# Two feed-forward layers: local attention's turns in another order, the second norm and the gated unit in one block, shifted copies by transfer

## The reference

```
def _layer(x, wqkv, qs, ksc, wo, lg, lb, w1, b1, w2, b2):
    h = shift_token(x)                     # channels 64..127 come from the token before
    q, k, v = split(h @ wqkv)              # 8 heads of 64
    q, k = l2norm(q) * qs, l2norm(k) * ksc
    q, k = rotary_xpos(q, k)
    o = local_attention(q, k, v)           # blocks of 64 tokens see themselves and the block before
    x = x + o @ wo
    h = shift_token(x)
    h = (h - mean(h)) / sqrt(var(h) + 1e-5) * lg + lb
    a, g = split(h @ w1 + b1)              # 341 each
    return x + (a * gelu(g)) @ w2 + b2
```

## Time and profile before

| | us |
|---|---|
| median of 3 runs (lowest, highest) | 1972.62 (1968.84, 1976.20) |
| the profiled execution | 1974.57 |
| its span | 1972.8 |
| layer 0: attention, norm, gated unit | 1098 to 1435, to 1461.2, to 1533 |
| layer 1: attention, norm, gated unit | 1533 to 1870, to 1897.7, to 1972.8 |

### The profile page before, as it was taken

How to read it: one execution, slowest core, us unless ns; L and a number is a source line. 1 busy time by engine, 2 the same in 40 slices (tenths; PEclk the granted TensorE clock), 3 DMA queues, 4 the chain that set the end, 5 groups by cost and what they waited for, 6 DMA issues and landing times. The chain is left out here.

```text
span 1972.8 us, 68063 instructions
## 1 busy us (share of the span) xinstructions
PE 1765.5 (89%) x28076; PEld 1051.8 (53%) x28076; DVE 1112.6 (56%) x3304; ACT 1487.9 (75%) x2649; POOL 425.4 (22%) x351
## 2 busy tenths in 40 slices
PE   8888899999999999999998788888879688888888
PEld 5664555555555555555554355555633355555533
DVE  5444533333333333333311699999853698989754
ACT  3333699999998999999998478887833587877733
POOL 1004000000000000000000556565300665565200
PEclk9988999999998999999999899998999899999999
DMA  1000311111111111111101201010000010010000
GB/s 56 3 3 24 113 51 53 59 46 58 50 56 42 58 58 58 59 58 46 42 16 55 57 18 25 16 23 14 17 1 0 20 25 18 18 23 13 18 11 32
DMA packets 42339, 69.60 MB, mean 35 GB/s; under 512 B 7377, under 2 KB 33105, under 8 KB 42065
## 3 DMA queue, kind: packets, MB, share of 16 engines
q1 hardware_dynamic: 42064, 65.66, 10.6%
HBM read 21.08 MB, written 2.10 MB: 12 GB/s over the span
## 5 line engine op out<-in xcount | busy, mean ns | idle before, releaser
L653 ACT ACTIVATE x_probs<-x_pss 128x1024 f32<-128x1024 f32 x832 | 806.4, 1021 | 51.7 <-PE x_pss L574 35.5
L588 PE MATMUL x_acc<-x_probs,x_v 128*32 128x256 f32 x6656 | 437.9, 380 | 0.1
L574 PE MATMUL x_pss<-x_qx,x_kx 32*128 32x256 bf16 x9984 | 348.4, 270 | 14.1 <-issue 6.3
L574 PEld LDWEIGHTS x_pss<-x_qx,x_kx 32*128 32x128 bf16 x9984 | 221.4, 93 | 199.8 <-ACT x_probs L653 180.3
L588 PEld LDWEIGHTS x_acc<-x_probs,x_v 128*32 128x32 f32 x6656 | 206.6, 110 | 93.5 <-issue 9.4
L1245 ACT ACTIVATE l_prob<-l_sim,l_neg_top,l_inv_norm 128x128 f32<-128x128 f32 x512 | 245.3, 485 | 0.4
L700 DVE COPY x_vnext<-x_psp 128x128 f32<-128x128 f32 (+1 forms) x199 | 59.1, 297 | 315.4 <-PE x_psp L552 312.3
L873 POOL TENSOR_TENSOR l_turned_half<-l_raw,l_tabB 128x512 f32<-128x512 f32 x128 | 160.2, 1272 | 155.7 <-ACT l_raw L1197 155.7
L629 POOL COPY x_zq<-zT 128x256 f32 (+1 forms) x15 | 6.0, 401 | 763.6 <-PE x_psp L559 695.4
L1149 DVE TENSOR_TENSOR l_prob<-l_prob,l_inv_total 128x512 f32<-128x512 f32 x128 | 157.5, 1231 | 4.4
L883 POOL TENSOR_TENSOR l_direct<-l_direct,l_turned_half 128x1024 f32<-128x1024 f32 x64 | 150.8, 2356 | 0.0
(11 more groups left out here) (172 smaller groups left out, 2826.7 us busy)
## 6 DMA issues: line engine op xcount, KB each, us to landing
x_kx<-x_kp SPq DMA_DIRECT2D x96, 208.0 KB, 2.3
x_cT<-in_context SPq DMA_DIRECT2D x16, 832.0 KB, 4.5
x_qx<-x_qp SPq DMA_DIRECT2D x48, 192.0 KB, 3.1
l_vmid<-l_vt SPq DMA_DIRECT2D x64, 128.0 KB, 2.3
xT<-in_x SPq DMA_DIRECT2D x8, 256.0 KB, 5.2
shifted<-zT SPq DMA_DIRECT2D x32, 64.0 KB, 2.0
out_x<-xT SPq DMA_DIRECT2D x8, 256.0 KB, 2.0
shifted<-zT SPq DMA_DIRECT2D x32, 63.8 KB, 2.0
```

The source lines that it names most:

```text
L574: ins = pe.matmul(pss[bank(k, 2 * p + r // 2)][:, r % 2, e, :], kx[par][rows, g, j * P:(j + 1) * P], qx[par][rows, g, a * S:(a + 1) * S], ...
L588: ins = pe.matmul(acc[32 * r:32 * r + 32, 0:S], v[:, j, g, r, :], probs[SLOT[p]][r // 2][:, r % 2, e, :], start=(u == 0), stop=(u == UNITS ...
L653: act.activation(probs[SLOT[p]][y][:, :, :, :], pss[bank(k, 2 * p + y)][:, :, :, :], ACT.Sigmoid, scale=HD ** -0.5).then_inc(weighed, 1)
```

## The change

**Local attention.** The `turn` of PE, ACT, DVE and POOL lists the same pieces in another order; some move to a neighbouring turn, as `mask(x, 0, 0)`, which is now the last of the turn before. `turn_halves` gets a wait on `joined`, since it may now run ahead of the join that reads its tile. SP gets `shift_sum`: once a row's sum is in `zT`, two transfers write its shifted copy into `hs` (`moved_to`). POOL clears the first token's upper half once per layer.

```
@@ local_attention, SP
+            def shift_sum(n):
+                sp.wait_ge(added, n + 1)
+                sp.dma_start(moved_to[0:64, n * S:(n + 1) * S], zT[0:64, n * S:(n + 1) * S]).then_inc(moved[n // 2], 16)
+                sp.dma_start(moved_to[64:P, n * S + 1:(n + 1) * S], zT[64:P, n * S:(n + 1) * S - 1]).then_inc(moved[n // 2], 16)
             for n in range(B):
                 middle(n)
                 if n + 4 < B:
                     shift(n + 4)
+                if n >= 3:
+                    shift_sum(n - 3)
+            for n in range(B - 3, B):
+                shift_sum(n)
@@ POOL
             def turn(x):
+                turn_halves(later(x, 1), 1)
+                join(later(x, 1), 0)
+                turn_halves(later(x, 2), 0)
                 scale_keys(later(x, 1), 0)
-                turn_halves(later(x, 2), 0)
                 join(later(x, 1), 1)
                 scale_keys(later(x, 1), 1)
-                turn_halves(later(x, 2), 1)
-                join(later(x, 2), 0)
@@ PE, the new order
+                score(x, 0)
+                project_q(later(x, 2), 0)
+                project_k(later(x, 2), 0)
+                project_v(x, 1)
+                turn_over(later(x, -1), 1, 0)
+                project_q(later(x, 2), 1)
+                value(later(x, -1), 0)
+                turn_over(later(x, -1), 1, 1, x)
+                score(x, 1)
+                value(later(x, -1), 1)
+                flip_q(later(x, 1), 0)
+                turn_over(x, 0, 0)
+                project_k(later(x, 2), 1)
+                project_out(later(x, -1))
+                flip_k(later(x, 1), 0)
+                flip_q(later(x, 1), 1)
+                turn_over(x, 0, 1)
+                flip_k(later(x, 1), 1)
+                project_v(later(x, 1), 0)
@@ DVE, the new order
+                norm(later(x, -1), 1, 1)
+                multiply_q(later(x, 2), 0)
+                multiply_k(later(x, 2), 0)
+                copy_v(x, 1)
+                mask(x, 0, 1)
+                floor_of(later(x, 1))
+                norm(x, 0, 0)
+                multiply_q(later(x, 2), 1)
+                inverse_norms(later(x, 1))
+                mask(x, 1, 0)
+                sums(later(x, 2), 0)
+                mask(x, 1, 1)
+                multiply_k(later(x, 2), 1)
+                norm(x, 0, 1)
+                place_keys(later(x, 1), 0)
+                add(later(x, -1))
+                norm(x, 1, 0)
+                place_keys(later(x, 1), 1)
+                sums(later(x, 2), 1)
+                copy_v(later(x, 1), 0)
+                mask(later(x, 1), 0, 0)
@@ ACT, the new order
+                exps(later(x, -1), 1, 1)
+                copy(later(x, -1), 0, 1)
+                copy_q(later(x, 2), 0)
+                copy_k(later(x, 2), 0)
+                exps(x, 0, 0)
+                squares(later(x, 2), 0)
+                copy_q(later(x, 2), 1)
+                copy(later(x, -1), 1, 0)
+                roots(later(x, 1))
+                copy_out(later(x, -1), 0)
+                copy(later(x, -1), 1, 1)
+                exps(x, 0, 1)
+                copy_out(later(x, -1), 1)
+                copy_k(later(x, 2), 1)
+                place_queries(later(x, 1), 0)
+                exps(x, 1, 0)
+                squares(later(x, 2), 1)
+                copy(x, 0, 0)
+                place_queries(later(x, 1), 1)
```

```
@@ norm_and_gate, PE (new)
+            fold()
+            for n in range(6):
+                mean_of(n)
+            variances(0)
+            for n in range(6, NCH):
+                mean_of(n)
+            variances(1)
+            pe.wait_ge(newton, run * NG * 2 + 2)
+            for c in range(4):
+                spread_out(0, c)
+            pe.wait_ge(newton, (run * NG + 1) * 2 + 2)
+            pe.wait_ge(centered, base + NCH)
+            chunks(pe, chunk)
+            narrow(NCH - 1, 1)
@@ its helpers
+            def mean_of(n):
+                pe.wait_ge(moved[n], 16 + 64 * (layer + 1))
...
+            def fold():
+                for m in range(2 * HC):
+                    ins = pe.matmul(wide[3][:, m:m + 1], w["w1"][:, m * P:(m + 1) * P], w["ln_b"][:, 0:1], start=True, stop=True)
+                ins.then_inc(folded, 1)
...
+            def widen(n, c):
+                if isinstance(n, int) and n == 0:
+                    pe.wait_ge(normed, base + (1, 1, 6)[c])
+                else:
+                    pe.wait_ge(gate_ready, passes + HC * (n - 1) + c + 1)
...
+            def chunk(n, u):
+                if isinstance(n, int) and n == 0:
+                    widen(0, 0)
+                    for c in range(4):
+                        spread_out(1, c)
+                    widen(0, 1)
+                    widen(0, 2)
+                else:
+                    if isinstance(n, int) and n == 1:
+                        pe.wait_ge(normed, base + NCH)
+                    widen(n, 0)
+                    narrow(n - 1, 1 - u)
+                    widen(n, 1)
+                    widen(n, 2)
@@ DVE (new)
+            dve.wait_ge(folded, layer + 1)
+            dve.tensor_tensor(bias[:, :], wide[3][:, 0:2 * HC], w["b1"][:, :], ALU.add).then_inc(bias_ready, 1)
+            for n in range(NCH):
+                dve.wait_ge(mean_ready, base + n + 1)
+                dve.tensor_tensor(hs[:, at[n]], hs[:, at[n]], mean[n % 2][:, :], ALU.subtract).then_inc(centered, 1)
+            refine(0)
+            scale(0)
+            refine(1)
+            for n in range(1, NCH):
+                scale(n)
+            chunks(dve, chunk)
+            add(NCH - 1)
```

More of the change, by code:

```diff
@@ L908, in _, with project_q @@
         def _(pe):
[L909 to L911 removed]
+            def project_q(x, t):
                 if exists(x):
@@ L1327, in narrow @@
             def narrow(n, u):
-                pe.wait_ge(gate_ready, HC * (n + 1))
-                if not isinstance(n, int) or n > 0:
-                    pe.wait_ge(added, n)
+                pe.wait_ge(gate_ready, passes + HC * (n + 1))
+                if isinstance(n, int) and n == 0:
+                    pe.wait_ge(normed, base + NCH)
+                else:
+                    pe.wait_ge(added, runs + n)
                 for c in range(HC):
@@ L1343, in _ @@
+            pe.wait_ge(newton, (run * NG + 1) * 2 + 2)
+            pe.wait_ge(centered, base + NCH)
             chunks(pe, chunk)
             narrow(NCH - 1, 1)
-        @block.scalar
-        def _(act):
-            with act.Fori(0, NCH) as n:
-                for c in range(HC):
-                    act.wait_ge(up, HC * n + c + 1)
-                    act.activation(gelu[c][:, :], psg[c][:, :], ACT.Gelu,
-                                   bias=w["b1"][:, HC + c:HC + c + 1]).then_inc(gelu_ready, 1)
@@ L1375, in chunk, with _, square_of, guess @@
                         add(n - 1)
-                    if c == 1 and (not isinstance(n, int) or n < NCH - 1):
-                        shift_by_bias(n + 1)
-            shift_by_bias(0)
+            dve.wait_ge(folded, layer + 1)
[8 more added lines that the diff above has]
+                scale(n)
             chunks(dve, chunk)
             add(NCH - 1)
+        @block.scalar
+        def _(act):
+            def square_of(n):
+                act.wait_ge(centered, base + n + 1)
+                act.activation(square[n][:, :], hs[:, at[n]], ACT.Square).then_inc(square_ready, 1)
+            def guess(g):
+                act.wait_ge(var_ready, run * NG + g + 1)
+                act.activation(rstd[g][:, :], var[g][:, :], ACT.Ln, bias=eps[:, 0:1]).then_inc(log_ready, 1)
+                act.wait_ge(log_ready, run * NG + g + 1)
+                act.activation(rstd[g][:, :], rstd[g][:, :], ACT.Exp, scale=-0.5).then_inc(guess_ready, 1)
+                act.wait_ge(guess_ready, (run * NG + g) * 2 + 1)
+                act.activation(rsquare[g][:, :], rstd[g][:, :], ACT.Square).then_inc(guess_ready, 1)
+            act.preload_act_table_set("natural_log_exp_and_others")
+            for n in range(6):
+                square_of(n)
+            guess(0)
+            for n in range(6, NCH):
+                square_of(n)
+            guess(1)
+            act.preload_act_table_set("gelu_and_others")
+            act.wait_ge(bias_ready, layer + 1)
+            with act.Fori(0, NCH) as n:
+                for c in range(HC):
+                    act.wait_ge(up, passes + HC * n + c + 1)
+                    act.activation(gelu[c][:, :], psg[c][:, :], ACT.Gelu,
+                                   bias=bias[:, HC + c:HC + c + 1]).then_inc(gelu_ready, 1)
 def build(nc, a, out):
@@ L1397, in build @@
         made = ctx.enter_context(nc.semaphore("made"))
+        moved = [ctx.enter_context(nc.semaphore(f"moved{n}")) for n in range(NCH)]
+        stored = ctx.enter_context(nc.semaphore("stored"))
+        gates = [ctx.enter_context(nc.semaphore(f"gate_{n}")) for n in (
+            "folded", "bias_ready", "up", "gelu_ready", "gate_ready", "down", "added")]
```

155 lines of the change are left out of this document (71 added, 84 removed).

## The result

| | us |
|---|---|
| median before (lowest, highest) | 1972.62 (1968.84, 1976.20) |
| median after (lowest, highest) | 1877.65 (1873.96, 1877.82) |
| ratio, 95% interval | 0.9513 (0.9479 to 0.9547) |
| profiled execution after, its span | 1873.96, 1872.1 |

The forecast was 1889, its range 1860 to 1935. The kernel became 11 us faster than forecast. Lines have moved: `norm` is now L1146 and L1148, `neg_top` L1138, the last `inverse_norms` L1119, `add` L1156; POOL's `turn_halves` L870, `join` L880, `scale_keys` L889; in the joint block the mean is L1336, `fold` L1341, the subtraction L1442, `widen` L1359, `narrow` L1370, the sum into `zT` L1424.

What follows compares the result with a forecast made beforehand. DVE was taken as the bound, held up by POOL's instructions in flight. Norm and gated unit 23.8, looped turns 55.9 and part-empty turns 4 sum to 83.7 us off 1974.6, 1890.9; median forecast 1889 us, range 1860 to 1935.

Steps and rivals of the forecast that it cites:

- 4.0 us of blocking a turn: Looped attention turns, layer 0: DVE operations with two SBUF inputs wait for POOL's instruction in flight, 4.0 us a turn.
- Part B: Looped attention turns: new orders shorten a turn from 20.18 and 20.28 to 17.9 us, gaining 55.9 us.
- norm(n,1,0): In the turn, due where POOL's first half-turn ends: loses 0.05 us meeting that boundary, 1.25 if not; taken as 0.65.
- Heads and tails: First four and last three attention turns, part empty: gain 2 us per layer, 4 in all (0 to 12).
- Part A: Norm and gated unit of both feed-forward layers: gain 23.8 us, from 20 to 27.
- One half-clock stretch per norm: First up products of the joint block: PE at half clock, some 1.7 us, kept in a gain of 7.2 us.
- its 8.8: Layer 1's norm: gain 8.8 us, since that norm is 1.5 us longer before the change.
- A second stretch per norm: Joint block without warm-up products: another slow PE stretch in each norm, making the gain there 20.4 instead of 23.8 us.
- ACT as the bound (1858): Looped turns: POOL's work falls almost wholly in the gaps, ACT bounds at 16.6 us a turn; 1858 us, chance 0.15.
- PE's clock on the path (1923): Looped turns: half clock ahead of products feeding ACT costs 1.4 us, turn 19.3, or blocking stays near 3; chance 0.23.
- The rivals with 3 us or more of blocking (1945, 1971): Turns: POOL's shorter groups block as much, 20.2 us, chance 0.07; or meet nearly all ten operations, 21.3 us, chance 0.05.
- random meetings: Upper case for the turn: ten sensitive DVE operations meet POOL at random, each losing 0.50 us, 5.0 in all; turn 21.3.

Runs made afterwards that it cites:

- the joint block alone: Changed kernel with the old orders of the turns, keeping only the joint block of norm and gated unit with shifted copies by transfer: 1952.2 us, ratio 0.9905.

## Why the prediction was right, and where it was off

**What bounds the kernel.** Right: DVE, by 4.0 us of blocking a turn. With POOL cut away the turn loses 3.75 us of its 4.0 blocked in layer 0 and 3.5 for 3.3 in layer 1. DVE's own work stays at 15.2 to 15.6 us a turn in every kernel here, and blocked and idle time make up the rest.

**Part B, the turn.** The forecast was 15.3 own + 1.0 idle + 1.6 blocked = 17.9. Layer 0: (196.34 - 10.9)/12 = 15.5 own, (204.30 - 196.34)/12 = 0.7 idle, 0.9 blocked, 17.0. The blocking was mis-sized by 0.7 us: all `neg_top` together took 0.29 a turn (priced at 0.5), norm(n,0,1) 0.17 (0.3), and norm(n,1,0) 0.45 (0.65): five misses at 1.07 over twelve turns. The norms and `inverse_norms` expected in POOL's pauses did lie there. Layer 1: 15.5 own, 1.3 idle, 1.0 blocked, 17.8. Of the idle 0.5 is two stalls. DVE stood 3.00 us and 2.84 us at the first norm's reciprocal. The second, and what the instruction queue did from 1677 to 1685:
```profile
1679.14 0.18 DVE L1146 RECIPROCAL l_inv_total<-l_total 128x4 f32<-128x4 f32 x1 [2.84 <-issue]
...
q14 instruction: 3, 0.02, 0.9%
```
The exponentials that this norm reads had ended by 1676.2, and nothing in the trace released it. PE then stood 3.54 us and took 2.07 instead of 1.12 for its next product; the turn took 22.75 us, the same turn of layer 0 16.85. Both stalls lie in the turn in which the loop goes back. All nine kernels here with the new order of DVE have two of 2.5 to 3.1 us, at that reciprocal, in layer 1 alone. With the old order it is `sums` that stands there, 1.2 to 2.2 us, twice in layer 1 (the joint block alone has none). In both orders that is the first piece of the turn, whatever it computes. An instruction fetch is my guess; layer 0 has packets on such queues too, without a stall, and no run tried it.

**Heads and tails.** Forecast 4, measured 7.3, nearly all of it in the heads. The 3.2 us ahead of the first feed-forward layer are in code that the change doesn't touch.

**Part A.** Right: 22.4 for 23.8. The steps of the joint block, by the timeline:
```profile
1390.80 1.47 PE L1341 MATMUL g_wide<-w_ln_b,w_w 128*128 128x1 f32 x12 [2.28 <-PEq L755]
...
1393.27 0.69 DVE L1442 TENSOR_TENSOR hs<-hs,g_mean 128x512 f32<-128x512 f32 x1 [0.80 <-PE g_mean L1336]
...
1427.91 0.75 DVE L1424 SCALAR_TENSOR_TENSOR zT<-g_wide,w_b,zT 128x512 f32 x1 [1.32 <-PE g_wide L1370]
1435.76 0.75 DVE L1424 SCALAR_TENSOR_TENSOR zT<-g_wide,w_b,zT 128x512 f32 x1 [1.33 <-PE g_wide L1370]
```
The last `add` ends at 1388.98: the first subtraction is 4.29 us later (forecast 4.3), `fold` 1.47 us (1.5), chunks are 7.85 apart (7.86). One half-clock stretch per norm was kept in the sum and one came per layer: in layer 0 at 1407.12, in layer 1 at the block's start, where the first three subtractions are 1.7 us apart. There the last subtraction is 3.1 us later behind the `add` than in layer 0; less the stretch that doesn't come behind it, that cost layer 1 about 1.5 us of its 8.8. Where such a stretch falls differs from trace to trace, and the old blocks vary too (97.9 to 100.4 us in layer 0): by the means of all traces part A is worth 12.2 + 11.1 = 23.3 us. A second stretch per norm did not come. The prediction's 20.4 us, worked out from the Trainium skill ("TensorE: Matmul & The Clock Gate", Part 1), was the case in which it does.

**Rivals.** ACT as the bound (1858) was near: 94% busy, and 16.6 us a turn is what the kernel takes without POOL. PE's clock on the path (1923): the opposite came, 1.00 in the turns. The slow `project_out`, 3.47 us, takes 1.99. The prediction called it slow once a turn; in the trace of before it took more than 2.1 us in 15 of 32 turns and 1.89 to 1.99 in the others. The mistake behind it was to read the old clock as PE's own trait in this loop, when it goes away with POOL's work. The rivals with 3 us or more of blocking (1945, 1971) fell; random meetings would have cost 5.0, and the order of the new lists is far from random. The Trainium skill's rule of one owner at a time ("SBUF — State Buffer", Who interferes with whom) agrees with the rows of both engines; with no slot at all between queued instructions, norm(n,1,0) would have missed in all turns, and it missed in 5 of 12.

## What to carry to other kernels

Price an order written by hand against the lock between DVE and POOL: list all DVE operations with two SBUF inputs, the small ones too, put POOL's groups on the same clock, and count only the rest of the POOL instruction in flight. Then measure the blocking in all of them: one list moved it from the norms into `inverse_norms`. To learn whether the lock or the chain is the cost, cut POOL's work to a few elements once; here that run named the whole cost (3.75 us a turn) and the next bound (ACT). Moving the shifted copies onto a queue with room, ahead of a serial block, gave about 4 us a layer and cost the turns nothing. Cutting POOL's instructions was a cheap substitute for the new order (1907.6 us against 1899.1), but not an addition to it.

## What was not expected of the hardware

- The lock goes both ways at boundaries: DVE's norm gets in between two POOL instructions at its full 0.69 us, and the POOL instruction behind it takes 1.78 us instead of 1.26. Which of the two goes first turned on less than 0.15 us, and cost 1.06 us.
- A product of only 4 elements a partition pays like a large one: `neg_top` took 0.72 us behind pieces of 256 elements.
- Cutting 1024 elements in four costs POOL 0.5 us (2.9 for 2.4).
- PE's granted clock over the turns rose from 0.94 to 1.00 when another engine's work was cut away, with PE's own order unchanged.
- DVE stood about 3 us in layer 1 where the loop goes back, with its inputs ready (1.2 to 2.2 us in the old order, at another piece, the first of its turn); layer 0 has no such stall. This is told, not explained.
